# LeViT-style attention block: V transposed by VectorE blocks and SBUF transfers, logits in float32

## The reference

```python
q = conv1x1_bn(x, qw, ...)      # 8 heads x 32
k = conv1x1_bn(x, kw, ...)      # 8 heads x 32
v4 = conv1x1_bn(x, vw, ...)     # 8 heads x 128 = 1024 channels
vl = depthwise_conv3x3(v4)      # then scale and shift
attn = einsum('bhid,bhjd->bhij', q, k) * SCALE + ab[:, BIAS_IDXS]
attn = einsum('bhij,gh->bgij', attn, th1w) + th1b     # heads mixed
attn = softmax(attn, axis=-1)
attn = einsum('bhij,gh->bgij', attn, th2w) + th2b     # heads mixed again
o = relu(einsum('bhij,bhjd->bhid', attn, v) + vl)
x = x + conv1x1_bn(o, pw, ...)  # back to 384 channels
```

## Time and profile before

| | us |
|---|---|
| median of 3 runs | 4813.25 (4812.56 to 4814.12) |
| the profiled execution | 4811.84 |
| its span, first to last instruction | 4810.0 |
| TensorE matmuls busy | 4779.1 (99%) |
| VectorE busy | 4175.9 (87%) |
| ScalarE busy | 3251.4 (68%) |
| GpSimd busy | 988.6 (21%) |

### The profile page before, as it was taken

One profiled execution on the slowest core, in us unless ns is written; L12 is line 12 of the kernel. 1 busy time (PEld: TensorE's weight loads), 2 busy tenths in 40 slices (PEclk: granted clock), 3 DMA queues, 4 the chain that ended last, 5 costly groups with the idle time before them and its releaser, 6 DMA issues.

```text
span 4810.0 us, 111468 instructions
## 1 busy us (share of the span) xinstructions
PE 4779.1 (99%) x35842; PEld 4760.2 (99%) x35842; DVE 4175.9 (87%) x10897; ACT 3251.4 (68%) x8005; POOL 988.6 (21%) x1093
## 2 busy tenths in 40 slices
PE   7999999999999999999999999999999999999999
PEld 7999999999999999999999999999999999999999
DVE  8888888889888898888888988889888888898887
ACT  6666666666667666667666666766666766666665
POOL 3212212121121221221212212122121221221211
PEclk9999999999999999999999999999999999999999
DMA  1000000000000000000000000000000000000000
GB/s 57 26 20 30 19 26 30 15 30 25 20 30 15 30 25 20 30 15 30 30 15 30 25 20 30 15 30 25 20 30 15 30 29 16 30 21 24 30 15 26
DMA packets 55148, 120.23 MB, mean 25 GB/s; under 512 B 3650, under 2 KB 5842, under 8 KB 55124
## 3 DMA queue, kind: packets, MB, share of 16 engines
q1 hardware_dynamic: 55124, 119.93, 7.4%
HBM read 81.38 MB, written 38.54 MB: 25 GB/s over the span
## 4 chain that ended last, share of the span: by engine, by line
PE 98%; DVE 1%; issue 0%; DMA 0%; ACT 0%; SPq 0%; DVEq 0%
PE psA L250 43%; PE psA L399 14%; PE psL L250 12%; PE psM L250 10%; PE psM L377 8%; PE psL L377 6%; PE psM L367 2%; PE psL L367 2%; DVE psC L620 1%; PE psA L268 0%; PE psA L263 0%; DMA qa<-in_wqkv 0%; DVE probs L675 0%; DVE x_lo L601 0%; DVE q_lo L650 0%
## 5 line engine op out<-in xcount | busy, mean ns | idle before, releaser
L620 DVE SCALAR_TENSOR_TENSOR psC<-vpad,par,psC 128x406 f32<-128x406 f32 x3072 | 1808.7, 637 | 0.0
L498 ACT ACTIVATE probs<-probs,nmax 112x196 f32<-112x196 f32 x1792 | 799.0, 449 | 649.0 <-DVE nmax L675 641.8
L250 PE MATMUL psA<-x_hi,w_lo 128*128 128x392 f32 x2304 | 795.0, 345 | 8.5 <-DVE x_lo L601 8.5
L250 PE MATMUL psA<-x_lo,w_hi 128*128 128x392 f32 x2304 | 788.9, 342 | 0.0
L250 PE MATMUL psA<-x_hi,w_hi 128*128 128x392 f32 x2304 | 788.1, 342 | 0.0
L399 PE MATMUL psA<-qa,shared 105*128 105x196 f32 x4096 | 693.9, 330 | 3.0 <-DVE shared L719 3.0
L399 PEld LDWEIGHTS psA<-qa,shared 105*128 105x128 f32 x4096 | 680.2, 191 | 3.3 <-DVE shared L719 3.3
L650 DVE SCALAR_TENSOR_TENSOR q_lo<-q,th,q_hi 128x392 fp32r<-128x392 f32 x1024 | 604.4, 621 | 34.6 <-ACT q_hi L442 27.6
L719 DVE TENSOR_TENSOR shared<-psA,shared 128x392 f32<-128x392 f32 x512 | 290.1, 567 | 366.5 <-PE psA L399 366.5
L442 ACT ACTIVATE q_hi<-q,th 128x392 fp32r<-128x392 f32 x1024 | 582.0, 620 | 6.0
L434 ACT ACTIVATE o_hi<-shared 128x392 fp32r<-128x392 f32 x512 | 271.5, 530 | 457.6 <-DVE shared L719 457.6
(11 more groups left out here) (85 smaller groups left out, 10500.0 us busy)
## 6 DMA issues: line engine op xcount, KB each, us to landing
xs<-in_x SPq DMA_DIRECT2D x64, 588.0 KB, 3.8
shared<-in_x SPq DMA_DIRECT2D x64, 588.0 KB, 3.8
out<-shared SPq DMA_DIRECT2D x63, 588.0 KB, 3.0
qa<-in_wqkv SPq DMA_DIRECT2D x3, 768.0 KB, 6.7
stage_wp<-in_wp SPq DMA_DIRECT2D x1, 1536.0 KB, 9.9
out<-shared SPq DMA_DIRECT2D x3, 196.0 KB, 2.0
shared<-in_abx SPq DMA_DIRECT2D x1, 165.4 KB
par<-in_par SPq DMA_DIRECT2D x1, 70.5 KB
```

Of the source, the lines that this page charges most:

```text
L250: last = nc.tensor.matmul(dst, w, r, start=(begin and n == 0), stop=(end and n == 2))
L498: nc.scalar.activation(row, row, ACT.Exp, bias=nmax[:, img, b:b + 1], scale=-1.0, accum_out=rowsum[:, img, b:b + 1]).then_inc(s_exp, 1)
L620: nc.vector.scalar_tensor_tensor(a if tap == 7 else sums, src, taps[:, c, TAPS[tap]:TAPS[tap] + 1], a if tap == 0 else sums, MUL, ADD).the ...
```

## The change

The transposes of V and their copies leave TensorE and ScalarE. VectorE transposes V of one image in one instruction, in blocks of 32 x 32 (`turn`), after the last scores: 8 channel tiles x 7 blocks of 32 pixels (of 210 padded pixels). A block lands in the 32 partitions in which its channels were; 28 DMAs per image on SP's queue (`move_turned`), each from 32 partitions to 32 others, in pieces of 32 float32, bring the blocks to the partitions of their pixels. TensorE waits for all moves of an image before it multiplies by it. The keys are cut into 96 and 114 padded pixels, where they were two times 105, and the two windows of the mixing matmuls are both 114 wide and overlap.

The logits are one float32 matmul per product where they were three float32r ones. ScalarE writes the mixed queries once in float32 (`mixed_query`); q_lo, k_hi and k_lo are gone. Six of the convolutions that stood after the scores stand after the two turns. The turned blocks lie in a tensor `front` over x_lo, q and k, so GpSimd's x_low waits for the moves of image 0.

```diff
+        front = sb("front", [P, 2 * BLOCKS * PART])
+        turned = front[:, :].rearrange("p (i b c n) -> p i b c n", i=2, b=BLOCKS, c=VT)
...
+            def move_turned(t, img):
+                sp.wait_ge(s_turned, 2 * t + img + 1)
+                for b in range(BLOCKS):
+                    jc, row = (0, b * BLK) if b * BLK < CUT else (1, b * BLK - CUT)
+                    for a in range(P // BLK):
+                        sp.dma_start(vt[row:row + BLK, img, jc, :, a * BLK:(a + 1) * BLK],
+                                     turned[a * BLK:(a + 1) * BLK, img, b, :, :]).then_inc(s_vt_in[img], 16)
             def step(t, first, last):
                 if not last:
                     sp.wait_ge(s_xhi, t + 1)
                     sp.wait_ge(s_xlo, t + 1)
                     load_x(t + 1)
+                for img in range(2):
+                    move_turned(t, img)
                 if not first:
                     store(t)
                 residual(t + 1)
...
-                pe.wait_ge(s_klo, 2 * (t + 1))
-                pe.wait_ge(s_qlo, 16 * (t + 1))
+                pe.wait_ge(s_qk_sb, 4 * (t + 1))
+                pe.wait_ge(s_qmix, 16 * (t + 1))
...
-                            mm = split3(logit_bank(n)[:, (b - b0) * PIX:(b - b0 + 1) * PIX],
-                                        q_lo[:, img * RES + b, kt, :], q_hi[:, img * RES + b, kt, :],
-                                        k_lo[:, kt, px], k_hi[:, kt, px], kt == 0, kt == QT - 1)
+                            mm = nc.tensor.matmul(logit_bank(n)[:, (b - b0) * PIX:(b - b0 + 1) * PIX],
+                                                  mixed_q[:, img * RES + b, kt, :], k[:, kt, px],
+                                                  start=(kt == 0), stop=(kt == QT - 1))
...
-                            mm = nc.tensor.transpose(mix_bank(use)[:, c * P:(c + 1) * P],
-                                                     vpad[:, 4 * cg + c, at_:at_ + HALF], ident[:, :])
...
+                                                  probs[0:HP + 1, img, 2 * n + b, jc * CUT:jc * CUT + REST],
...
-                    pe.wait_ge(s_vt_sb, 8 * t + 4 * img + 4)
+                    pe.wait_ge(s_vt_in[img], 16 * MOVES * (t + 1))
...
+                def turn(img):
+                    at_ = PITCH + 1 + img * PITCH * PITCH
+                    nc.vector.transpose(turned[:, img, :, :, :].rearrange("p b c k -> p c b k"),
+                                        vpad[:, :, at_:at_ + BLOCKS * BLK].rearrange("p c (b k) -> p c b k", b=BLOCKS)
+                                        ).then_inc(s_turned, 1)
...
-                mixed_low(8)
-                convs(6)
-                for _ in range(8):
-                    mixed_low(1)
-                    convs(1)
-                convs(1)
+                convs(15)
...
-                convs(3)
+                turn(0)
                 dve.wait_ge(s_exp, 28 * t + 28)
                 nc.vector.reciprocal(rinv[:, 1, :], rowsum[:, 1, :]).then_inc(s_rinv, 1)
-                convs(3)
+                turn(1)
                 if not first:
                     project_out(t, 2)
                 convs(64)
...
-                    pool.wait_ge(s_v_mm, VT * (t + 1))
+                    wait_alone(pool, s_vt_in[0], 16 * MOVES * (t + 1))
                     x_low(t + 1)
```

More of the change, by code:

```diff
@@ L18 @@
 PITCH = RES + 1
-HALF = RES // 2 * PITCH
+KEYS = RES * PITCH
+BLK = 32
+BLOCKS = -(-KEYS // BLK)
+CUT = 3 * BLK
+REST = KEYS - CUT
+PART = VT * BLK
 HR = P // KD
@@ L29 @@
 EPS = 1e-5
+Q_AT = 2 * CT * PIX
+K_HI_AT = Q_AT + QT * COLS
+K_AT = K_HI_AT + QT * COLS
 GAP = 2 * RES * QT * HP - VT // 2 * ACC - 4 * DH
@@ L76, in build @@
         x_hi = sb("x_hi", [P, 2, CT, PIX], f32r)
[L77 to L83, removed]
+        x_lo = over("x_lo", [P, 2, CT, PIX])
+        front = sb("front", [P, 2 * BLOCKS * PART])
         qa = sb("qa", [P, 4 * RES * HP])
-        probs = sb("probs", [P, 2, RES, 2 * HALF])
+        probs = sb("probs", [P, 2, RES, KEYS])
         nmax = sb("nmax", [HP, 2, RES])
@@ L346, in step @@
                     project(t, 2, True)
-                def bank_free(use):
+                for use in range(14):
+                    img, n = divmod(use, 7)
                     if use < 4:
                         pe.wait_ge(s_score, 28 * t + 22 + 2 * use)
[L352 to L355, removed]
-                    else:
-                        pe.wait_ge(s_mix_sb, 14 * t + 7 * i + n + 1)
@@ new lines, in step @@
+                    else:
+                        pe.wait_ge(s_mix_sb, 14 * t + use - 3)
+                    pe.wait_ge(s_exp, 28 * t + 14 * img + 2 * n + 2)
+                    pe.wait_ge(s_mixw, 8 * t + 4 * img + group(2 * n + 1) + 1)
+                    bank = mix_bank(use)[:, 0:4 * HP].rearrange("p (j g b i) -> p j g b i", j=2, g=NH, b=2)
+                    for jc in range(2):
+                        for b in range(2):
+                            mm = nc.tensor.matmul(bank[:, jc, :, b, :],
+                                                  probs[0:HP + 1, img, 2 * n + b, jc * CUT:jc * CUT + REST],
+                                                  mixw[0:HP + 1, img, 2 * n + b, :].rearrange("p (g i) -> p g i", g=NH),
+                                                  start=True, stop=True)
@@ L397, in step @@
                             g = 2 * n + e
-                            for jc in range(2):
+                            for jc, rows in enumerate((CUT, REST)):
                                 mm = nc.tensor.matmul(psA[:, u % 2, e * PIX:(e + 1) * PIX],
-                                                      vt[0:HALF, img, jc, g * D:(g + 1) * D], attn[:, img, jc, g, :],
+                                                      vt[0:rows, img, jc, g, :],
+                                                      attn[0:rows, img, jc, g, :],
                                                       start=(jc == 0), stop=(jc == 1))
@@ L502, in step @@
                         conv_centre(t, CENTRES[n])
[L503 to L516, removed]
+                for use in range(14):
+                    img, n = divmod(use, 7)
+                    act.wait_ge(s_mix_mm, 14 * t + use + 1)
+                    if use == 0 and not first:
+                        act.wait_ge(s_av_mm, 8 * t)
+                    src = mix_bank(use)[:, 0:4 * HP].rearrange("p (j g m) -> p j g m", j=2, g=NH)
+                    nc.scalar.copy(attn[:, img, :, :, 2 * n * RES:(2 * n + 2) * RES], src).then_inc(s_mix_sb, 1)
+                    if use == 6 and not last:
                         act.wait_ge(s_v_mm, VT * (t + 1))
@@ L774, in step @@
             def step(t, first, last):
-                for kt in range(QT):
-                    wait_alone(pool, s_khi, 2 * t + kt + 1)
-                    nc.gpsimd.tensor_tensor(k_lo[:, kt, :], k[:, kt, :], k_hi[:, kt, :].bitcast(f32),
-                                            SUB).then_inc(s_klo, 1)
                 if not last:
@@ L809, in triple @@
         return np.concatenate([tiles(a[f("q")]), tiles(a[f("k")]), tiles(a[f("v")])], axis=1)
-    eye = np.eye(P, dtype=np.float32)
     member = (np.arange(P)[:, None] // (GC // CT) == np.arange(GROUPS)[None, :]).astype(np.float32)
```

48 lines of the change are left out of this document (21 added, 27 removed).

## The result

| | before | after |
|---|---|---|
| median of the runs, us | 4813.45 | 6249.95 (6247.91 to 6253.51) |
| ratio | | 1.2985, 95% interval 1.2963 to 1.3008 |
| span of the profiled execution, us | 4810.0 | 6249.8 |

A forecast was written before the change was run, and what follows sets the result against it. The prediction took TensorE, 98% of the chain, as the bound; 4.6 (moves ending last) + 2.1 (logits) + 2.1 (clock) = 8.8 us a round, x 64 = 563, gave 5375 us, range 4950 to 5950.

The forecast's parts named there:

- logits: TensorE's logits: 56 float32 products a round take 18.6 us instead of 16.5, 2.1 us more.
- a turn: VectorE's transpose of one image's V after the logits: 2.04 us, taken from the nearest row, w_lo.
- landing: Time from the issue of an image's last 32 KB move to its arrival: 2.0 us.
- image 0 starts: First image's moves all landed at L+16.7, 1.6 us after TensorE is ready, covered by its later wait for VectorE.
- image 1 starts: Second image's half of attention times V starts when its moves end, L+28.5 against L+23.9 before: +4.6 us a round.
- clock: TensorE's granted clock drops after idles in the new round: 2.1 us lost a round, ends 0 and 2.7.
- 0.42 a move: SP's issue of each move after turn(0): 0.373 plus a gap of 0.05, ends 0.41 and 0.50.
- Case A: The forecast itself: SP's issue sets the moves' pace; 5375 us, own range 5210 to 5700, chance 0.58.
- Rival B: DMA engines, or what feeds them, are slower than SP with such pieces: 5920 us at 0.57 a move, chance 0.20.
- Mixing: TensorE's mixing matmuls: stationary window grows from 105 to 114 columns, costed at nothing, at most 0.9 us a round.
- Rival C: Moves hide and VectorE's late convolutions decide when attention times V runs: 2.3 us a round, 4960 us, chance 0.13.
- Rival D: TensorE's own order stays the bound and 1.4 us a round come out: 4722 us, chance 0.08.

The follow-up runs named there:

- logits alone: The kernel before with only the float32 logits, q_lo, k_hi and k_lo gone, V still transposed by TensorE: 4936.63 us, ratio 1.0256.
- the route experiment: Changed kernel with seven small DMAs ahead of each image's moves, differing in route and partitions: 6805.69 us, measured once.
- the kernel with bigger pieces: Changed kernel with V laid out so that a move is 32 pieces of 1 KB instead of 256 of 128 bytes: 6358.88 us, ratio 1.3213.
- the kernel with three moves of four: Changed kernel leaving out the moves of channels 96 to 127 from the second round on, 42 a round instead of 56: 5683.58 us, ratio 1.1809.
- the kernel with one move: Changed kernel with a single move per image from the second round on, all other links kept: 5285.66 us, ratio 1.0983.

## Why the prediction was wrong in size and right in mechanism

Measured in the round of the profile above. L is the end of the last record of the logits, as 2456.08 was: here 3073.50 (the last 16 records start at 3070.68 and take 2.82).

| step | forecast | measured |
|---|---|---|
| logits | 18.6 a round, +2.1 | +1.93 (logits alone) |
| first move issued | L+3.4 | L+3.3 |
| a turn | 2.04 | 2.01 |
| landing | 2.0 | 1.96 |
| a move | 0.42, ends 0.41 and 0.50 | **0.654** |
| image 0 starts | L+16.7 | L+23.0 |
| image 1 starts | L+28.5 | L+41.5 |
| clock | 2.1, ends 0 and 2.7 | 2.55 |
| a round, over before | 8.8 | 22.5 |

**The failed step is the term "0.42 a move".** Case A is what happened: SP's issue paces the moves, and every link of its chain but this one came out. From the first issue to the start of the last, the forecast had 55 x 0.42 = 23.1; it was 36.0 (3076.83 to 3112.84). That is 12.9 us, x 64 = 826 of the 875 us missed. The clock adds (2.55 - 2.1) x 64 = 29, the start of image 1's half (0.1 later than these terms give) 8, the logits take back 11. Another 11 are in the forecast's L+23.9 for the kernel before, a time of the chain; the record of that half starts at L+23.7. That leaves some 11 us, not assigned.

Why 0.42 was wrong: it was the duration of L207 with a gap of 0.05. That is a DMA over 128 partitions out of device memory; in the route experiment the issue alone takes 0.42 for such a one and 0.59 for 32 partitions within SBUF. The range's upper end failed as well, and that was avoidable: 0.50 was about the *mean* distance of the 14 start-up issues, while two of the single rows were longer. SP's queue at start-up, kernel before:

```profile
1.75 0.42 SPq L211 DMA_DIRECT2D g_bc<-in_g_bc  x1
...
4.10 0.71 SPq L218 DMA_DIRECT2D th<-in_th  x1
4.85 0.60 SPq L218 DMA_DIRECT2D small<-in_small  x1
5.50 0.43 SPq L218 DMA_DIRECT2D shared<-in_abx  x1
```

The longest row, 0.71 and 0.75 to the next start, gives 5375 + 55 x 0.33 x 64 = 6537 by the same sum, so a range with that end would have held the result; the measured 0.65 gives 6185. A factor that is multiplied by 55 x 64 must take its end from the longest single row, not from an average.

**Rival B** gave 5920 at 0.57 a move, near the result, but for another reason: DMA engines slower than SP, landings ever later. Landings stayed at 1.96, and pieces of 16 bytes cost as much as pieces of 1 KB, so B did not happen. The rule of the Trainium skill that the prediction weighed ("DMA: Bandwidth & Descriptors", Specifications: transfers under 512 bytes as read-modify-write) does not set the time here: moves of 128-byte pieces took 0.65 with a landing of 2.0, moves of 1 KB pieces 0.63 with 1.9. But the pace is SP's, so it cannot show what a piece costs the DMA engines. Their busy share can: while the moves run it is 0.34 (3080 to 3112) with 128-byte pieces and 0.22 (3036 to 3068 in the kernel with bigger pieces) with 1 KB pieces. So the exemption of SBUF to SBUF (same page, "Why small descriptors are slow (HBM only)") is not borne out in full: small pieces keep the engines busy half as long again for the same bytes, and it costs nothing only because they wait for SP two thirds of the time.

**Mixing.** The wider window was costed at nothing. The mixing costs a little more: 16 records now start 1.60 apart where 16 took 1.53, 0.5 us a round, hidden in the changed kernel by the wait behind it. The window alone was not tested.

**Clock.** 2.1 came from the first round, and 2.55 was inside its ends. There, 2.14 us of idle had been followed by the slow level; here 2.28 was, and 1.14 and 0.84 were not. Between 2 and 3 us the length of the idle alone does not decide. In the kernel with three moves of four, TensorE waits 2.95 ahead of image 0 in 61 rounds; in 11 of them its half then ran at full clock (5.65, as here), in the others it did not (7.28 at 3088.41):

```profile
707.64 5.65 PE L396 MATMUL psA<-qa,shared 96*128 96x196 f32 x32 [2.96 <-DMA shared<-front]
```

**Rival C** is what remains when the moves vanish, and its 4960 lacked two prices: the clock, and x_low beside the convolutions. Those two put the kernel with one move at 5286.

**Rival D** was right as a mechanism and blocked only by the order. Its gain, 4722 in the prediction, plus the 0.5 of the mixing x 64 = 32, is 4754; turned early and with VectorE's gap filled, the same change measured 4753.38, with all 56 moves at 0.65 in it. That it meets the sum within 1 us is in part luck: the logits took 1.93 where the sum has 2.1, which is 11 us.

## What to carry to other kernels

Many small DMAs on one queue cost their issue, one after another, whatever their size: multiply the count by a duration of an issue of the same form (partitions, route) in a loop, and where the trace has none, let the range reach to its longest row. Before work is moved behind the last producer, look whether it can stand ahead of it: here 36.6 us of moves a round cost 1340 us behind the logits, with the clock that their waits slow, and nothing beside them. When an instruction is moved away from a place, ask what wait it had been covering there, and put other work in it.

## What the runs showed of the hardware

- SP's issue inside the loop: 0.37 to 0.42 over 128 partitions between device memory and SBUF, 0.54 over 128 within SBUF, 0.59 to 0.60 over 16 to 64 partitions within SBUF, 0.58 over 32 out of device memory; pieces of 16 bytes to 1 KB, 32 to 256 of them, change it by under 0.03 each. Why height matters is not settled, and it is not a simple rule. At start-up one DMA over 32 partitions (g_bc) took 0.42 and one over 128 (th, 64 bytes in each) 0.71; two into one partition took 0.33 or less, and of two over 112 partitions one took 0.43, the other 0.60.
- The DMA engines' busy share while a move of 32 KB is issued every 0.65 or 0.63: 0.34 with pieces of 128 bytes, 0.22 with pieces of 1 KB.
- VectorE's transpose in 32 x 32 blocks: 1792 float32 per partition in 2.01 us, 1.12 ns an element, near the 1.14 of the two-operand w_lo; with an output stride of 8 elements 3.58.
- Two convolutions from SBUF beside a GpSimd subtraction from SBUF: 3.86 us instead of 1.17, longer by about as long as that instruction ran (2.68). Convolutions with one operand in PSUM took their usual 0.63 beside it.
- TensorE's granted clock stayed at 1.00 behind idle times of 0.84 and 1.14 us, and was at 0.50 to 0.59 (the 1.2 GHz level for most of it) in the stretches shown behind 2.28, 5.64, 7.53 and 10.56 us. Behind 2.95 us it was full in 11 rounds of 61 and fell in 50.
